# The first block table made one iteration ahead, and block 0's products placed before the last attention output

## The reference

```
x = x + attn(layernorm(x))
  attn(x): xn = x / rms(x); u, v, base = split(silu(xn @ uv_w.T))   # 256, 256, 128
           q, k = rope(base * gamma + beta)
           out = (u * (relu((q k^T + w_rel) / sqrt(128))**2 @ v)) @ o_w.T
           return x * res_scale + out
x = x + ffn(layernorm(x))
  ffn(x):  xn = layernorm(x) * gamma + beta; probs = softmax(xn @ Wr + br)   # 8 experts
           scores, idx = top_k(probs, 2)
           expert_e = relu(xn @ W1[e] + b1[e]) @ W2[e] + b2[e]                # hidden 512
           return x + sum over the two of score * (expert_idx - c_idx + c_total)
```

## Time and profile before

| | |
|---|---|
| median of 3 runs | 356.28 us |
| profiled execution | 356.23 us, span 354.2 us |
| TensorE (PE) busy | 314.9 us, 89% of the span |
| VectorE (DVE) busy | 238.2 us, 67% |
| ScalarE (ACT) busy | 239.5 us, 68% |
| GpSimd (POOL) busy | 190.0 us, 54% |
| chain that ended last | PE 49%, POOL 12%, issue 12%, DVE 11%, ACT 11%, DMA 3% |
| mean granted TensorE clock | 0.976 |

### The profile page before, as it was taken

One profiled execution on the slowest core, in us unless ns is written; L12 is line 12 of the kernel. 1 busy time (PEld: TensorE's weight loads), 2 busy tenths in 40 slices (PEclk: granted clock), 3 DMA queues, 4 the chain that ended last, 5 costly groups with the idle time before them and its releaser, 6 DMA issues.

```text
span 354.2 us, 7616 instructions
## 1 busy us (share of the span) xinstructions
PE 314.9 (89%) x2031; PEld 255.1 (72%) x2031; DVE 238.2 (67%) x739; ACT 239.5 (68%) x466; POOL 190.0 (54%) x193
## 2 busy tenths in 40 slices
PE   1279999999999999999996879999999999999940
PEld 1167657575756647575653779999999999999940
DVE  1578548888787778879869466785555555556843
ACT  1455948969798796979654348677777777776710
POOL 7150305136667586647658077657776455455460
PEclk9999999999999999999999699999999999999995
DMA  6983100000101010010101232323333322239518
GB/s 161 306 296 88 44 0 2 0 0 24 39 8 45 10 38 23 25 38 8 55 15 46 60 94 68 93 70 85 106 103 99 95 71 74 61 81 332 164 41 237
DMA packets 33403, 28.39 MB, mean 80 GB/s; under 512 B 5399, under 2 KB 28868, under 8 KB 33364
## 3 DMA queue, kind: packets, MB, share of 16 engines
q1 hardware_dynamic: 25634, 16.43, 16.6%
q0 software_dynamic: 4320, 8.47, 7.2%
q10 hardware_dynamic: 3410, 3.03, 3.2%
HBM read 16.75 MB, written 11.61 MB: 80 GB/s over the span
## 4 chain that ended last, share of the span: by engine, by line
PE 49%; POOL 12%; issue 12%; DVE 11%; ACT 11%; DMA 3%; SPq 1%; POOLq 0%; ACTq 0%; DVEq 0%
PE B_o L855 17%; PE B_uv L844 17%; POOL slots L455 6%; PE B_o L794 4%; ACT xs L540 2%; PE B_m L718 2%; ACT gswap L582 2%; ACT acc L540 2%; ACT s_rel L564 2%; PE B_o L785 2%; POOL rs L446 1%; DVE go L1045 1%; PE B_S L769 1%; ACT gbase L576 1%; ACT th_u L525 1%
## 5 line engine op out<-in xcount | busy, mean ns | idle before, releaser
L486 POOL DMA_INDIRECT y<-u,xb x71 | 70.4, 992 | 47.6 <-ACT u L654 37.1
L855 PE MATMUL B_o<-W2s,K 128*128 x568 | 75.3, 276 | 2.3 <-DVE K L1203 2.3
L455 POOL DMA_INDIRECT slots<-rows,pos x64 | 64.8, 1013 | 18.6 <-issue 17.3
L855 PEld LDWEIGHTS B_o<-W2s,K 128*128 128x128 f32 x568 | 69.0, 192 | 2.8 <-issue 2.7
L785 PE MATMUL B_o<-K,v 128*128 128x512 f32 x128 | 59.3, 596 | 0.0
L643 ACT ACTIVATE t<-W1s 128x644 f32 x36 | 26.6, 740 | 21.9 <-DVE yd L1209 21.3
L844 PE MATMUL B_uv<-xbT,t 128*128 128x128 f32 x288 | 38.1, 275 | 0.0
L1203 DVE TENSOR_TENSOR K<-B_uv,t 128x512 f32<-128x512 f32 x36 | 24.8, 692 | 18.4 <-PE B_uv L844 18.2
L785 PEld LDWEIGHTS B_o<-K,v 128*128 128x128 f32 x128 | 22.9, 190 | 19.8 <-issue 18.2
L844 PEld LDWEIGHTS B_uv<-xbT,t 128*128 128x128 f32 x288 | 35.1, 192 | 0.0
L773 PE MATMUL B_S<-G,ident_r 128*128 128x512 f32 x64 | 32.9, 594 | 0.0
(11 more groups left out here) (197 smaller groups left out, 653.4 us busy)
## 6 DMA issues: line engine op xcount, KB each, us to landing
xb<-slots SPq DMA_DIRECT2D x71, 65.0 KB, 1.9
x_all<-L_attn_x SPq DMA_DIRECT2D x8, 256.0 KB, 3.1
W1s<-L_ffn_W SPq DMA_DIRECT2D x1, 2048.0 KB, 11.7
x_all<-y SPq DMA_DIRECT2D x4, 512.0 KB, 6.4
out<-acc SPq DMA_DIRECT2D x6, 256.0 KB
y<-u,xb POOLq DMA_INDIRECT x71, 2.3
slots<-rows,pos POOLq DMA_INDIRECT x64, 2.4
slots<-zrow SPq DMA_DIRECT2D x9, 65.0 KB, 2.9
```

Source lines behind the costliest of these rows:

```text
L455: pool.indirect_dma_start(out=slots, out_offset=bass.IndirectOffsetOnAxis(ap=pos[:, q % 2, c:c + 1], axis=0), in_=rows[:, q % 2, c // T, c ...
L486: pool.indirect_dma_start(out=y2, out_offset=bass.IndirectOffsetOnAxis(ap=xb[:, k, D:D + 1].bitcast(u32), axis=0), in_=yb[:, k, :], in_off ...
L855: last = nc.tensor.matmul(B_y[n % 2], hT[:, n % 2, c * P:(c + 1) * P], W2s[:, bass.ds(w + c * D, D)], start=(c == 0), stop=(c == T - 1))
```

## The change

It does the following.

- `table_a` covers 33 blocks, full blocks of batches 0 to 4 (FIRST = 5). The count of those five batches and DVE's first step (the copy out of PSUM) are done in iteration 6, the other 15 steps in iteration 7. `row_tab` is then complete for the first 33 blocks without batch 5's counts, and SP waits for the scatters of batches 0 to 4 only.
- The counts of batches 0 to 5, from which the segments are made, are a second count in iteration 7, with seven steps of their own (`segments`). A third count serves `table_b`, which has 38 blocks.
- The residual of batch 7 is done on DVE (`last_residual`), between the table and the segments.
- TensorE in iteration 7: block_rows(0), block_rows(1), hidden(0), output, prefix of batch 6. DVE: gate of batch 7, top of batch 6, relu of block 0, softmax. ACT: the weights of block 0 before exps of batch 6.
- Batch 7's scatter is threaded from put 11 on instead of 12, the zeroing of the tails stands ahead of load 29 instead of 32.

```diff
-OLD = 6
-FULL = OLD * L * TOPK // P
-NA = FULL - (NE - 1)
-NB1 = ((FULL - NA) * P + NE * (P - 1)) // P
+FIRST, OLD = 5, 6
+NA = FIRST * L * TOPK // P - (NE - 1)
+NB1 = (OLD * L * TOPK - NA * P + NE * (P - 1)) // P
-TABA, TAIL_AT, TABB = 17, 2, 21
+TABA, TAIL_AT, TABB = 16, 2, 21
-SCATTER_AT, TAILS_AT, ADD_AT = 12, 32, 61
+SCATTER_AT, TAILS_AT, ADD_AT = 11, 29, 61
...
             sp.wait_ge(tabA_step, TABA)
-            sp.wait_ge(scattered[0], 16 * TOPK * T * (OLD // 2))
-            sp.wait_ge(scattered[1], 16 * TOPK * T * (OLD // 2))
+            sp.wait_ge(scattered[0], 16 * TOPK * T * ((FIRST + 1) // 2))
+            sp.wait_ge(scattered[1], 16 * TOPK * T * (FIRST // 2))
...
                 if a == BATCH - 1:
                     scatter(r - 1, q)
-                    residual(a, q)
...
                 if r is not None:
                     residual_of_ffn(r)
+                if a == BATCH - 1:
+                    weights_of(0)
...
-            for n in range(2):
-                weights_of(n)
-                block_input(n)
+            block_input(0)
+            weights_of(1)
+            block_input(1)
...
+                if a == BATCH - 2:
+                    count(0, FIRST)
                 if a == BATCH - 1:
-                    count(0, OLD)
+                    count(1, OLD)
...
+                if a == BATCH - 2:
+                    te.wait_ge(tabA_step, 1)
                 if a == BATCH - 1:
-                    te.wait_ge(tabA_step, 1)
+                    te.wait_ge(seg_known, 1)
...
-                if r is not None:
+                if r is not None and n is not None or a == BATCH - 2:
                     prefix(r)
                 if a == BATCH - 1:
                     block_rows(0)
                     block_rows(1)
+                    hidden(0)
                 if a is not None:
                     output(a)
+                if a == BATCH - 1:
+                    prefix(r)
...
+            def segments():
+                dve.wait_ge(cnt_ps, 2)
+                link(cp(cnt[:, :], B_m[:, 0:NE]))
+                yield
+                link(ts(cnt_i[:, 1, :], cnt[:, :], float(P - 1), None, ALU.add))
+                link(ts(nb_i[:, 1, :], cnt_i[:, 1, :], 7, None, ALU.arith_shift_right))
+                link(cp(nb[:, 1, :], nb_i[:, 1, :]))
+                link(tt(seg[:, 0:NE], nb[:, 1, :], full[:, :], ALU.subtract))
+                link(stt(seg_row[:, 0:NE], full[:, :], float(P), region8[:, :], ALU.mult, ALU.add))
+                link(stt(seg_row[:, NE:], nb[:, 1, :], float(P), region8[:, :], ALU.mult, ALU.add))
+                yield
+
+            def last_residual(q):
+                dve.wait_ge(z_ready, BATCH)
+                tt(z[:, q % 2], z[:, q % 2], res_rep[:, :].unsqueeze(1).broadcast_to([P, T, D]),
+                   ALU.mult).then_inc(res_step, 1)
+                dve.wait_ge(res_step, 2 * BATCH - 1)
+                tt(res[:, :, :], z[:, q % 2], x_all[:, tok(BATCH - 1), :], ALU.add).then_inc(res_step, 1)
...
+                if a == BATCH - 2:
+                    next(first_table)
                 if a == BATCH - 1:
-                    table_a()
+                    next(first_table)
+                    next(rest)
+                    next(first_table)
+                    last_residual(q)
+                    next(rest)
...
+                if a == BATCH - 1:
+                    gate(a, q)
                 if r is not None:
                     top(r)
+                if a == BATCH - 1:
+                    hidden_relu(0)
+                if r is not None:
                     softmax(r, q + 1, link)
-                if a is not None:
-                    gate(a, q)
+                if n is not None or a == BATCH - 2:
+                    if a is not None:
+                        gate(a, q)
```

More of the change, by code:

```diff
@@ L197, in build_layer @@
         gen_b = th_v[:, 0:NB * 2 * NE].rearrange("p (n e) -> p n e", n=NB)
-        blk_e = sb("blk_e", [P, NA])
-        blk_s = sb("blk_s", [P, NA])
-        blk_r = sb("blk_r", [P, NA])
+        blk_e = sb("blk_e", [P, max(NA, NB)])
+        blk_s = sb("blk_s", [P, max(NA, NB)])
+        blk_r = sb("blk_r", [P, max(NA, NB)])
         row_tab = sb("row_tab", [P, NBLK], i32)
@@ L597, in copy_rows, with weights_of, block_input, weighted @@
                 nc.scalar.activation(rows[:, q % 2, 1, :, 0:D], rows[:, q % 2, 0, :, 0:D], ACT.Copy).then_inc(xn_copied, 1)
+            def weights_of(n):
+                if n == 0:
+                    act.wait_ge(tabA_step, TABA)
+                    act.wait_ge(s_ld_w1, 16)
+                if n == NA:
+                    act.wait_ge(tabB_step, TABB)
+                e = act.value_load(d_tab[0:1, n:n + 1], min_val=0, max_val=(NE - 1) * WROW)
+                after(act, yd_ready, n - 3)
+                nc.scalar.activation(W1c[n % 4], W1s[:, :, :].rearrange("p e w -> p (e w)")[:, bass.ds(e, WROW)],
+                                     ACT.Copy).then_inc(W1c_ready, 1)
+            def block_input(n):
+                act.wait_ge(xbT_ps, n + 1)
+                after(act, h_ps, n - 1)
+                nc.scalar.activation(xbT[:, n % 2, :], B_T[n % 2], ACT.Identity, bias=fb_col[:, :],
+                                     scale=fg_col[:, :]).then_inc(xbT_ready, 1)
+            def weighted(n):
+                act.wait_ge(yd_ready, n + 1)
+                nc.scalar.activation(yb[:, n % NSLOT, :], yd[:, n % 2, :], ACT.Copy,
+                                     scale=xb[:, n % NSLOT, D + 1:D + 2]).then_inc(y_ready, 1)
             for n, p, a, r, q in pipeline(act):
@@ L920, in _ @@
                 if n == COUNT_AT:
-                    count(1, BATCH)
+                    count(2, BATCH)
         @block.vector
@@ L1135, in table_a @@
                 tab(cp(cnt[:, :], B_m[:, 0:NE]))
+                yield
                 tab(cp(cnt_i[:, 0, :], cnt[:, :]))
-                tab(ts(cnt_i[:, 1, :], cnt[:, :], float(P - 1), None, ALU.add))
-                tab(ts(nb_i[:, :, :], cnt_i[:, :, :], 7, None, ALU.arith_shift_right))
-                tab(cp(nb[:, :, :], nb_i[:, :, :]))
+                tab(ts(nb_i[:, 0, :], cnt_i[:, 0, :], 7, None, ALU.arith_shift_right))
+                tab(cp(nb[:, 0, :], nb_i[:, 0, :]))
                 tab(tt(cumw[:, 0:NE, 0:NE], upto[:, 0:NE, 0:NE], nb[:, 0:1, :].broadcast_to([P, NE, NE]), ALU.mult))
@@ L1143, in table_a @@
                 tab(tt(full[:, :], taken[:, 1:NE + 1], taken[:, 0:NE], ALU.subtract))
+                yield
                 tab(tt(ge_a, blk_id[:, 0:NA].unsqueeze(2).broadcast_to(pne),
                        taken[:, 1:NE + 1].unsqueeze(1).broadcast_to(pne), ALU.is_ge))
-                tab(red(blk_e[:, :], ge_a, AX, ALU.add))
+                tab(red(blk_e[:, 0:NA], ge_a, AX, ALU.add))
                 tab(tt(gen_a, ge_a, full[:, :].unsqueeze(1).broadcast_to(pne), ALU.mult))
-                tab(red(blk_s[:, :], gen_a, AX, ALU.add))
@@ L1149, in table_a @@
[L1149 to L1154, removed]
@@ L1155, in table_a @@
-                stt(seg_row[:, NE:], nb[:, 1, :], float(P), region8[:, :], ALU.mult, ALU.add).then_inc(seg_ready, 1)
+                tab(red(blk_s[:, 0:NA], gen_a, AX, ALU.add))
+                tab(stt(blk_r[:, 0:NA], blk_s[:, 0:NA], -float(P), blk128[:, 0:NA], ALU.mult, ALU.add))
+                tab(stt(row_tab[:, 0:NA], blk_e[:, 0:NA], float(REGION), blk_r[:, 0:NA], ALU.mult, ALU.add))
+                tab(ts(w_tab[:, 0:NA], blk_e[:, 0:NA], float(F), None, ALU.mult))
+                assert tab(ts(d_tab[:, 0:NA], blk_e[:, 0:NA], float(WROW), None, ALU.mult)) == TABA
@@ new lines, in table_a, with link @@
+                yield
+            def segments():
+                count = [0]
+                def link(ins):
+                    count[0] += 1
+                    ins.then_inc(seg_known, 1)
+                    dve.wait_ge(seg_known, count[0])
+                dve.wait_ge(cnt_ps, 2)
+                link(cp(cnt[:, :], B_m[:, 0:NE]))
+                yield
+                link(ts(cnt_i[:, 1, :], cnt[:, :], float(P - 1), None, ALU.add))
[4 more added lines that the diff above has]
+                link(stt(seg_row[:, NE:], nb[:, 1, :], float(P), region8[:, :], ALU.mult, ALU.add))
+                yield
@@ L1165, in table_b @@
                 pns = [P, NB, 2 * NE]
-                dve.wait_ge(cnt_ps, 2)
-                dve.wait_ge(seg_ready, 3)
+                dve.wait_ge(cnt_ps, 3)
                 tab(cp(cnt[:, :], B_m[:, 0:NE]))
@@ L1224, in _ @@
             dve.wait_ge(s_pool0, POOL0)
+            first_table, rest = table_a(), segments()
             for n, p, a, r, q in pipeline(dve):
@@ L1276, in _ @@
                     expert_sum(n - 2)
-                if n < NBLK:
+                if 0 < n < NBLK:
                     hidden_relu(n)
```

4 lines of the change are left out of this document (2 added, 2 removed).

## The result

| | before | after |
|---|---|---|
| median | 356.47 us (356.17 to 356.88, 4 runs) | 348.55 us (348.25 to 348.80, 4 runs) |
| ratio after/before | | 0.9777 (95% interval 0.976 to 0.9794) |
| profiled execution, span | 356.23 us, 354.2 us | 348.46 us, 346.6 us |
| mean granted clock | 0.976 | 0.987 |

The prediction was 349.0 us (348.0 to 351.2). The medians are 7.9 us apart, the profiled executions 7.8, the spans 7.6; the working had 7.25. The busy time of stretches after the change, with the columns of the earlier trace rows (the engines are PE, PEld, DVE, ACT, POOL): first a one-microsecond stretch of PE's old pause, then the short pause that is left, then the block phase.

What follows compares the result with a forecast made beforehand. The prediction took TensorE's never-idle block phase, and so its late start after attention, to bound the kernel. Saving 7.9 - 0.5 - 0.15 = 7.25 us from 356.23 gave 349.0 us, range 348.0 to 351.2.

Steps and rivals of the forecast that it cites:

- Part 1: First table a batch earlier: iteration 6 costs 0 (bounds 0 and 1.1 us), table ready at 188.0.
- Part 2: Residual on DVE, 0.70 us a step: logits 0.45 us later, at 190.7; the cast beginning top two gains 1.66 us.
- Rival B: Residual on DVE held up by POOL's scatter tiles, up to 0.96 us each: 350.9 us, chance 0.07.
- Part 3: Block 0 first at the hand-over: expert_out(0) at 197.65, 7.9 us sooner; 0.5 comes back at relu(1).
- Part 4: Second table in the block phase, 38 blocks instead of 30: costs 0.15 us (0 to 0.7).
- Part 5: Scatter and zeroed tails sooner: loads 29 and 33 fit by 1.0 us or more, cost 0.
- Rival D: Block stream outruns its loads, so slower: 360.8 us with ten POOL turns of lateness, chance 0.04.
- The sum: Whole kernel: 7.9 - 0.5 - 0.15 = 7.25 us saved from 356.23, giving 349.0 us, chance 0.72.
- A: PE's clock falls at its pause before hidden(0), 3.0 us less 0.5 lost: 351.5 us, chance 0.08.
- C: Iteration 6 pays its 1.1 us and the second table 0.7 instead of 0.15: 350.65 us, chance 0.06.
- E: No change, the saved time is waited off later at a step that doesn't move: 356.2 us, chance 0.03.

Runs made afterwards that it cites:

- Experiment 6: The changed kernel with batch 7's residual back on POOL, early, and relu(1) ahead of batch 6's positions on DVE: 347.12 us against 356.23 before, ratio 0.975.
- experiment 4: The changed kernel with relu(0) back in the block loop, behind batch 6's positions: 352.03 us against 356.15 for the kernel before, ratio 0.9896.
- experiment 3 in full: The kernel before with unused products filling nearly all of PE's pause: 388.2 us against 388.56 without them, on a disturbed chip, ratio 0.9998.
- experiment 1: The changed kernel with block 0's products and weights, gate, top two and relu(0) in their old order: 351.76 us against 356.23 before, ratio 0.9896.
- experiment 3: The kernel before with seven unused products in PE's pause: 356.11 us against 356.15 without them, ratio 0.9998.
- experiment 5: The changed kernel with batch 7's residual back on POOL, but early in iteration 7: 347.91 us against 356.15 for the kernel before, ratio 0.9775.

## Why the prediction was right

Point by point, by its own steps.

- **Part 1, iteration 6**: cost 0, as taken. The copy ended at 167.03 (167.1), and the waits up to rope_sin hid it. The table was ready at 187.93 (188.0).
- **Part 2**: the residual took 0.69 + 0.69 us (0.70 each), with POOL's scatter tiles beside it. Rival B falls. Its price rested on scatter tiles blocking a product of two SBUF tensors, which no row here shows. The Trainium skill ("SBUF — State Buffer", Who interferes with whom), on whose rule of blocking the prediction drew, adds as an inference that tensor_tensor takes only the read side of the shared ports while a DMA's descriptor generation needs the write side; the 0.69 us agree with that. The logits started at 190.62 (190.7), and the cast took 0.16 us (0.17). The prediction priced the gain on the cast alone, 1.66 us; the last step of top two gained too, 1.13 us before and 0.19 after, but its 0.7 us for top two had that in it.
- **Part 3**: hidden(0) at 192.73 (192.85), x1 at 195.69 (195.9), relu(1) at 199.13 (199.35), expert_out(1) at 199.96 (200.05). expert_out(0) was at 197.13 instead of 197.65: I had given the steps from the output product on 0.4 us too much. So 8.4 us were saved there and not 7.9, and 0.8 came back at relu(1), not 0.5: 207.55 - 199.96 = 7.6 by the start of expert_out(1). Experiment 6 takes these 0.8 us back, so they were where the prediction had them. The "about 6 us" of PE's work at full clock were nearer 5 (from 191.47 to 197.13 are 5.66 us, 0.82 of them waiting), but nothing in the sum used them.
- **Part 4**: the second table's wide steps took 0.78 us (at most 0.82 worked out), and cost nothing that can be seen. With the same wait in front, one sum of DVE stands at 241.17 before and at 233.51 after, 7.66 apart, no less than the 7.6 at expert_out(1):

Before, then after, timeline of DVE behind the second table:

```profile
241.17 0.29 DVE L1209 TENSOR_TENSOR yd<-B_o,t 128x128 f32<-128x128 f32 x1 [0.21 <-PE B_o L855]
```

```profile
233.51 0.29 DVE L1239 TENSOR_TENSOR yd<-B_o,t 128x128 f32<-128x128 f32 x1 [0.21 <-PE B_o L855]
```

- **Part 5**: no wait for blocks 29 and 33. SP's queue and PE of the changed kernel, against the earlier trace rows:

```profile
234.79 8.08 SPq L311 DMA_DIRECT2D slots<-zrow  x8
243.63 65.69 SPq L348 DMA_DIRECT2D xb<-slots  x42
```

```profile
249.37 0.27 PE L837 MATMUL B_S<-ident,xb 128*128 128x128 f32 x1
```

  Load 29 was issued at 243.63, ahead of the bounds of 244.3 to 246.2, and PE took block 29 at 249.37 (249.1). Landed by 245.5, with the median 1.9 us of these loads, it has a slack of 3.8 us, where I had bounds of 1.0 to 2.9. The last scatter tile went on POOL at 245.14 and load 33 at 248.67, landed by 250.6 (254.1 at the latest), and PE took block 33 at 256.96 (256.6). Rival D had less ground than I gave it.
- **The sum**: the terms add up to 8.4 - 0.8 = 7.6, the difference of the spans; the forecast was 0.35 short, 0.2 of it in the steps around the output product net of what came back, 0.15 in the second table. That it came so near is in part luck: 0.5 us too little at expert_out(0) and 0.3 too little for what comes back have opposite signs. Outside the span lie 1.86 us instead of the 2.03 that I kept, another 0.17.
- **Rivals**: A did not come about, since PE's pauses were 0.56 and 0.26 us, and later 0.77; experiment 4 shows that it was one step away. The 2.5 us I gave it were too much: a fall cost 1.64 us there, and the old one 1.7 (experiment 3 in full). I had halved all 6 us of slow clock, though up to 197.62 PE waited for rows in any case, and only the work behind them could lose by it. C and E didn't occur: iteration 6 paid nothing and the end moved with the start.

What the prediction did not say is how the parts share the gain. The early table, with the residual, has 4.5 us, the order 0.6 by itself and 2.8 more on top of it.

## What to carry to other kernels

Where a long phase runs at one engine's pace, its start is all there is to gain, and the start is found by following each engine's queue to the first instruction of that phase: here four different waits (rows, top two, output product, relu) lay behind one another, and taking away one alone gave 4.5 or 0.6 us of 7.9. After each saving, ask which small step still stands behind an unrelated long one; two such steps gave another 1.3 us in the trace. A pause on TensorE can cost more than its length: one of 2.65 us cost 1.64 us more in clock (experiment 4), one of 2.30 us nothing (experiment 1). So a step that shortens or splits a long pause can be worth more than the waiting it saves.

## What the runs showed of the hardware

The clock and the pauses of TensorE: it kept its full clock over a pause of 2.3 us (before, until 205.55, and experiment 1, until 200.70), and lost it in experiment 4 after one of 2.65 us, and there one microsecond after work had begun again. In experiment 3 it fell without any pause above 1.91 us. So neither the length of one pause nor being at work decides by itself. The Trainium skill ("TensorE: Matmul & The Clock Gate", Part 1) has the clock follow how busy the engine has been, which experiment 3 in full bears out: with unused products in the pauses the clock stayed at 1.00, where before it had fallen to 0.51. How much work is enough these runs don't settle.

A cast on DVE of 8 numbers per partition took 1.83 us beside POOL's multiply and 0.16 us without it; a small product of DVE took 1.13 us beside POOL's sum and 0.19 without it. DVE's 128x512 products took 0.69 us each beside POOL's scatter tiles. The residual in POOL's idle time (experiment 5, 178.72 to 179.99) ran beside DVE's statistics of batch 6 and left the logits where they were expected.

On two of the chips the same kernel took 9 to 10% longer, and the traces taken there have instructions late on every engine. Only timing in turns with the kernel before on the same chip keeps such a number from being read as an effect.
